# Output projection and first layer norm: applying the norm of one token group inside the matmul loop of the next

## The reference

```python
def _layernorm(x, axis=-1, eps=1e-5):
    m = jnp.mean(x, axis=axis, keepdims=True)
    v = jnp.var(x, axis=axis, keepdims=True)
    return (x - m) / jnp.sqrt(v + eps)

# x: (4, 4096, 4096)
x = _layernorm(x + _L0_attn_ref(x, ...))   # 8 heads of 64, ends in out @ Wo_w.T + Wo_b
x = _layernorm(x + _L0_ffn_ref(x, ...))    # dense 4096x4096 + top-2-of-8 LoRA experts
```

## Time and profile before

| | us |
|---|---|
| median of 13 runs | 4233.42 (4199.22 to 4473.61) |
| time of the profiled execution | 4216.77 |
| its span on the slowest core (core 7) | 4215.2 |
| spans of the 8 cores | 4149.0 to 4215.2 |
| busy on core 7: PE, DVE, ACT, POOL | 3192.0, 1367.2, 826.2, 714.9 |

### The profile page before, as it was taken

One profiled execution on the slowest core, in us unless ns is written; L12 is line 12 of the kernel. 1 busy time (PEld: TensorE's weight loads), 2 busy tenths in 40 slices (PEclk: granted clock), 3 DMA queues, 4 the chain that ended last, 5 costly groups with the idle time before them and its releaser, 6 DMA issues.

```text
span 4215.2 us, 46281 instructions; the slowest of 8 cores (4149.0 to 4215.2 us)
## 1 busy us (share of the span) xinstructions
PE 3192.0 (76%) x13476; PEld 1204.8 (29%) x13476; DVE 1367.2 (32%) x1908; ACT 826.2 (20%) x1412; POOL 714.9 (17%) x567
## 2 busy tenths in 40 slices
PE   4776795968888887888888655450799997999960
PEld 3555342412222222222222111110344442444420
DVE  0000000055566656566556235553100002111124
ACT  1222000013333333333333322110000000000000
POOL 2111101000000000000000013334222221444425
PEclk9998898956777767677767677775899998999985
DMA  8998545400000000000000142213554544666637
GB/s 245 284 280 263 158 137 167 135 11 1 1 1 3 1 1 1 3 1 1 3 1 1 36 132 75 80 40 98 175 160 148 162 133 155 201 209 204 208 116 191
DMA packets 450639, 444.75 MB, mean 106 GB/s; under 512 B 21472, under 2 KB 402529, under 8 KB 450402
## 3 DMA queue, kind: packets, MB, share of 16 engines
q1 hardware_dynamic: 347490, 341.12, 27.3%
q10 hardware_dynamic: 102912, 100.68, 7.4%
HBM read 340.01 MB, written 100.66 MB: 105 GB/s over the span
## 4 chain that ended last, share of the span: by engine, by line
PE 56%; DVE 9%; issue 6%; DMA 5%; POOL 3%; ACT 0%; DVEq 0%; SPq 0%; POOLq 0%; ACTq 0%
PE pf L155 23%; PE sS L155 10%; PE rb L155 9%; PE a L155 7%; DVE racc L557 4%; PE po L155 3%; DVE x2g L965 2%; DMA outT<-outst 2%; POOL tmpf L955 2%; PE pstQ L155 1%; PE pstS L155 1%; DMA wstgo<-woT 1%; PE pss L155 1%; PE sS L582 1%; PE psq L155 1%
## 5 line engine op out<-in xcount | busy, mean ns | idle before, releaser
L557 DVE TENSOR_REDUCE racc<-sS 128x1 f32<-128x512 f32 x1024 | 681.9, 689 | 1260.5 <-PE sS L155 1247.1
L155 PE MATMUL pf<-x2h,wqf 128*128 128x512 bf16 x4096 | 909.8, 380 | 5.8 <-DVE hs L1285 5.8
L703 ACT ACTIVATE probs<-rb 128x512 bf16<-128x512 f32 x1024 | 541.9, 598 | 913.1 <-PE rb L155 910.2
L155 PE MATMUL sS<-kT,qT 64*128 64x512 bf16 x1024 | 476.1, 484 | 155.9 <-DVE racc L557 118.9
L155 PEld LDWEIGHTS pf<-x2h,wqf 128*128 128x128 bf16 x4096 | 396.7, 98 | 505.7 <-issue 39.5
L155 PE MATMUL a<-probs,V 128*65 128x512 bf16 x1024 | 376.9, 495 | 0.0
L155 PE MATMUL pk<-xbf,wk_bf 128*128 128x256 bf16 x2048 | 264.2, 289 | 139.8 <-ACT xbf L333 60.5
L1310 POOL CAST wqf<-wstgf 128x1024 bf16<-128x1024 f32 x256 | 264.5, 1040 | 581.3 <-DMA wstgf<-wbT 419.3
L1376 DVE SCALAR_TENSOR_TENSOR res2c<-pf,bB_sb,x2h 128x1024 bf16<-128x1024 f32 x64 | 82.2, 1284 | 865.1 <-PE pss L155 793.3
L155 PE MATMUL rb<-qT,kT 64*128 64x512 bf16 x1024 | 339.8, 474 | 0.4 <-PE rb L155 0.2
L844 POOL CAST wo_bf<-wstgo 128x1024 bf16<-128x1024 f32 x16 | 16.6, 1040 | 1702.5 <-DMA wstgo<-woT 1702.5
(11 more groups left out here) (104 smaller groups left out, 1763.1 us busy)
## 6 DMA issues: line engine op xcount, KB each, us to landing
wstgf<-wbT SPq DMA_DIRECT2D x256, 512.0 KB
xstg<-xrot SPq DMA_DIRECT2D x128, 512.0 KB
xscr<-xbf ACTq DMA_DIRECT2D x128, 256.0 KB, 5.5
xvb<-xscr SPq DMA_DIRECT2D x128, 256.0 KB, 2.7
outT<-outst ACTq DMA_DIRECT2D x64, 512.0 KB, 4.7
xqb<-xscr SPq DMA_DIRECT2D x32, 512.0 KB, 3.4
xq<-xscr SPq DMA_DIRECT2D x32, 512.0 KB, 3.6
x2scr<-x2g ACTq DMA_DIRECT2D x32, 512.0 KB, 2.8
```

The costliest lines, as they stand in the source:

```text
L155: return lambda e: e.matmul(o, l, r, start=st, stop=sp, skip_group_check=True)
L557: e.reduce_max(d, srd, AX.X, negate=True),
L703: e.activation(d, srd, AF.Exp),
```

## The change

The apply loop is no longer emitted behind its own group. The broadcast with its two copies, each of the 32 apply steps and each of the 8 DMAs to `x2scr` becomes a closure in a list `opend`. In the matmul loop of the next group, every step takes two of them off the list before it emits its own matmuls: 41 closures, so the first 20 of the 32 steps take two each and the next takes the last one. What is left in the list after the fourth group is emitted behind the loop. Beside that, the `po` tiles go from two to three, the `sq` tiles from two to four, the statistics matmuls trail by three steps in place of one, and the weights are loaded and tracked by column block (`hh` outside, `c` inside), so that a step waits only for the quarter of `wo_bf` that it reads.

```diff
-                woR = [Res() for _ in range(4)]
+                woR = [[Res() for _ in range(4)] for _ in range(4)]
-                sq = sbP("sq", [128, 2 * 512], BF16)
+                sq = sbP("sq", [128, 4 * 512], BF16)
-                for c in range(4):
-                    for hh in range(4):
-                        st_i = hh % 2
+                for hh in range(4):
+                    for c in range(4):
+                        st_i = c % 2
...
-                    po = [po0, po1]
+                    po = [po0, po1, po2]
+                    opend = []
...
                         for mc in range(NDC):
-                            pi = mc % 2
+                            for _ in range(2):
+                                if opend:
+                                    opend.pop(0)()
+                            pi = mc % 3
...
-                                    woR[hp_].rd() + OTr[hp_][qg].rd(),
+                                    woR[hp_][mc // 8].rd() + OTr[hp_][qg].rd(),
...
+                            if len(ppend) > 2:
+                                emit_stats(*ppend.pop(0))
...
-                            sqi = mc % 2
+                            sqi = mc % 4
...
                             ppend.append((mc, te, ts, sqi))
-                            if len(ppend) > 1:
-                                emit_stats(*ppend.pop(0))
...
+                        def mk_bcast(ro=ro, trs=trs, tb2=tb2):
+                            def f():
+                                tba = s.op("PE", mm(pbc0[:], ones1f[:], ro(1),
...
+                        opend.append(mk_bcast())
                         for mc in range(NDC):
...
+                            def mk_apply(mc=mc):
+                                def f():
+                                    ti = mc % 2
+                                    t1 = s.op("POOL",
...
+                            opend.append(mk_apply())
+                            if mc % 4 == 3:
+                                def mk_spill(qg=qg, g=mc // 4):
...
+                                opend.append(mk_spill())
+                    while opend:
+                        opend.pop(0)()
```

More of the change, by code:

```diff
@@ L819, in build_program @@
                 resR = [Res() for _ in range(32)]
-                sq = sbP("sq", [128, 2 * 512], BF16)
-                sqR = [Res(), Res()]
+                sq = sbP("sq", [128, 4 * 512], BF16)
+                sqR = [Res() for _ in range(4)]
                 x2g = sbP("x2g", [128, 32 * 512], BF16)
@@ L949, in build_program @@
-                        bbcR.did_write(tcb)
-                        for mc in range(NDC):
[L951 to L981, removed]
+                        def mk_bcast(ro=ro, trs=trs, tb2=tb2):
+                            def f():
+                                tba = s.op("PE", mm(pbc0[:], ones1f[:], ro(1),
+                                                    True, True),
+                                           waits=[trs] + pbcR_[0].wr() +
+                                           consts_fence)
+                                rowsRes[1].did_read(tba)
+                                pbcR_[0].did_write(tba)
+                                tbb = s.op("PE", mm(pbc1[:], ones1f[:], ro(0),
+                                                    True, True),
+                                           waits=[tb2] + pbcR_[1].wr())
+                                rowsRes[0].did_read(tbb)
+                                pbcR_[1].did_write(tbb)
+                                tca = s.op("DVE", lambda e, d=abc[:], srd=pbc0[:]:
+                                           e.tensor_copy(d, srd),
+                                           waits=[tba] + abcR.wr())
+                                pbcR_[0].did_read(tca)
+                                abcR.did_write(tca)
+                                tcb = s.op("DVE", lambda e, d=bbc[:], srd=pbc1[:]:
+                                           e.tensor_copy(d, srd),
+                                           waits=[tbb] + bbcR.wr())
+                                pbcR_[1].did_read(tcb)
+                                bbcR.did_write(tcb)
+                            return f
@@ new lines, in build_program, with f @@
+                        opend.append(mk_bcast())
+                        for mc in range(NDC):
+                            def mk_apply(mc=mc):
+                                def f():
+                                    ti = mc % 2
+                                    t1 = s.op("POOL",
+                                              lambda e, d=tmpf[ti][:],
+                                              a=res[:, mc * 512: mc * 512 + 512],
+                                              b=abc[:]:
+                                              e.tensor_tensor(d, a, b, ALU.mult),
+                                              waits=resR[mc].rd() + abcR.rd() +
+                                              tmpfR[ti].wr())
+                                    resR[mc].did_read(t1)
+                                    abcR.did_read(t1)
+                                    tmpfR[ti].did_write(t1)
+                                    t2 = s.op("DVE",
+                                              lambda e,
+                                              d=x2g[:, mc * 512: mc * 512 + 512],
+                                              a=tmpf[ti][:], b=bbc[:]:
+                                              e.tensor_tensor(d, a, b, ALU.add),
+                                              waits=[t1] + bbcR.rd() +
+                                              x2gR[mc].wr())
+                                    tmpfR[ti].did_read(t2)
+                                    bbcR.did_read(t2)
+                                    x2gR[mc].did_write(t2)
+                                return f
+                            opend.append(mk_apply())
+                            if mc % 4 == 3:
+                                def mk_spill(qg=qg, g=mc // 4):
+                                    def f():
+                                        tw = s.op("ACT",
+                                                  lambda e, qg=qg, g=g:
+                                                  e.dma_start(
+                                                      x2scr_r[
+                                                          :, 4 * g:4 * g + 4,
+                                                          qg * 512:
+                                                          qg * 512 + 512],
+                                                      x2g.ap().rearrange(
+                                                          "p (c n) -> p c n",
+                                                          c=32)[
+                                                          :, 4 * g:4 * g + 4, :]),
+                                                  waits=[tk for j in range(4)
+                                                         for tk in
+                                                         x2gR[4 * g + j].rd()],
+                                                  dma="sca")
+                                        for j in range(4):
+                                            x2gR[4 * g + j].did_read(tw)
+                                        x2scrR[qg].did_write(tw)
+                                    return f
+                                opend.append(mk_spill())
```

22 lines of the change are left out of this document (4 added, 18 removed).

## The result

The changed kernel takes 4122.88 us in the median of 11 runs, where 4119 were forecast. Over all runs that were compared, its time is 0.9756 of the kernel before, with a 95% interval of 0.9728 to 0.9784. In some executions of either kernel the cores of a die (0 to 3, or 4 to 7) run at a lower clock; every ratio here leaves these out, while the median of 11 runs includes two of them, and the other nine have 4113.31 in their middle. The profiled execution took 4113.44 us, 103.3 less than the one before; 104.6 were forecast for it.

A forecast was written before the change was run, and what follows sets the result against it. Apply and matmul loops, taking turns, bound the stage: 104.4 of 112.6 us a group. Three times 33.1 (99.3) plus 5.3 gave 104.6 off 4216.77, 4112.2; from the runs' middle, 4223.37, 4119. Range 4092 to 4173, the forecast's own 4100 to 4138.

The forecast's parts named there:

- What goes: Groups 2 to 4: apply and matmul loop together take 71.3 us in place of 104.4, 33.1 less a group.
- The 20 residual steps: Residual steps interleaved with the 32 applies: 2 us added to 52.6; contention rival 15 us, 4158 in all, chance 0.14.
- the nearer row: FFN residual operation beside POOL's weight cast, at its usual 1.28 and 1.04 us; taken as model for interleaved residual steps.
- the other end of the range: Interleaved residual steps all serial with the multiplies, contending like the add: 20 x 0.75 = 15 us; chance 0.14.
- the 1 us that would have spoken against the account: Interleaved steps: POOL idle longer than 1 us per pair would show the prediction wrong.
- The last 12 steps: Matmul-loop steps left without applies: 1.50 us a step, the loop ending at 69.3 before the clock allowance.
- the matmuls of steps 20 to 22 are done: At the end of residual step 19 (54.6), thanks to three po tiles; so step 23's matmuls start at 55.4.
- The clock: TensorE's granted clock: 2 us a group added in case the 12 steps without applies begin at the lower level.
- the sum of 71.3: Apply and matmul loop of one group together after the change: 69.3 plus 2 for the clock, in place of 104.4.
- The rival of a low clock: TensorE stays at the lower level through groups 2 to 4: only 16.4 us gained a group, 4169; chance 0.16.
- The first group: Group 1's matmul loop: step 31 starts at 2503.4 in place of 2508.66, a gain of 5.3 us.
- steps 4 to 6 are done on PE by then: Group 1, at residual step 4 (2466.53): step 7 then starts at 2467.4 and later steps take 1.50 each.

The follow-up runs named there:

- e2: Changed kernel with the deferral kept and the look-ahead taken back (two po and sq tiles, statistics one step late): interval 83.0 us, profiled execution 4123.31 us, no ratio.
- e3: Changed kernel with ScalarE copying each po tile to SBUF, so the residual step has two SBUF inputs: interval 89.6 us, ratio 0.9875 to the kernel before.
- e7: Changed kernel with the weights loaded in the old order, row block outside: interval 79.3 us, read by its trace alone.
- e4: Changed kernel with the add reading the broadcast row in PSUM, copy to bbc left out: ratio 0.9597 to the kernel before, median 4059.5 us.

## Why the prediction came out

- **What goes.** One apply loop beside one matmul loop, three times: forecast 33.1 a group, measured 112.8 - 79.3 = 33.5. e2 shows that the deferral carries 29.8 of it. That forecast and measurement agree so closely is in part luck, as the next three points show.
- **The 20 residual steps.** Put at 2 us, between -4 and 15. In the changed kernel residual step 19 ends 55.6 after the first multiply, against 52.6 + 2: 3 us. The choice of the nearer row (one input in PSUM, rows 6 and 7) was right, and e3 shows that the other end of the range is something that does happen, although not all of its 89.6 - 79.3 = 10.3 us need be contention. POOL waited 14.3 us for adds in this part, 0.89 a pair, under the 1 us that would have spoken against the account. The Trainium skill (SBUF — State Buffer, Who interferes with whom) says that a VectorE instruction with two SBUF inputs contends with a GpSimd instruction that reads SBUF, the later one waiting for the whole of the earlier, and that one with at most one such input, outside the two-port modes, doesn't; e3 and the changed kernel agree, up to 1652 ns with two and at most 752 with one.
- **The last 12 steps.** 1.49 a step against 1.50. The step that failed is "the matmuls of steps 20 to 22 are done": with three tiles only 20 and 21 are. (For the first group the same prediction counted rightly: step 7 starts when the tile of step 4 is free.) It cost 0.9 us (57.3 against 55.4, less the 1.0 by which residual step 19 was later).
- **The clock.** 2 us were put in for the case that the last 12 steps begin at the lower level, and none did: 1.00 there. The 0.95 of the interleaved part is a group's start: PE begins a group at the lower level, is busy without a break while it works ahead, and then has the upper level for the rest of the group. So the sum of 71.3 was met at 71.1 by luck, by two misses of opposite sign, 1.9 too little and 2 too much. The rival of a low clock is refuted: PE was busy for 27.84 of 48 us, in bursts, and stayed at the upper level. The Trainium skill (TensorE: Matmul & The Clock Gate, HAM oscillation) warns of matmuls in bursts, with waits for DMA between them, that start cold; pauses such as the 1.57 us ahead of 2573.49 and the 1.71 ahead of 2600.89 did not bring that, and the 1.67 and 2.96 us of e3, close behind each other, did.
- **The first group.** Forecast 5.3. First load to broadcast copy is 107.5, and it was 114.1 before (core 7: its stage begins at 2403.83, its first multiply at 2518.74, 0.8 behind the copy): 6.6. Here too two misses cancel, as the rows shown with e7 tell. The forecast left residual step 4 at 2466.53, because it waited for `xq`. But its own matmuls had ended only 0.17 us before that (2465.32 + 1.04), so PE paced it as well, and with the look-ahead it comes 5.9 us behind the first residual step in place of 9.3, 3.4 earlier (the row names `xq` again, but there too its matmuls had ended only 0.18 before, at 2495.69). From there to residual step 31 it takes 40.3 us in place of 43.3, a gain of 3.0 and not 5.3: "steps 4 to 6 are done on PE by then" failed, since step 5's matmuls begin only at 2496.15. Over the eight cores, first load to copy is 110.5 to 114.8 before and 101.4 to 107.6 now. That the weights' order brings nothing is shown by e7.
- **The rest.** The last apply loop stayed at 53 us, and nothing behind the barrier took the gain back: the sum of three times 33.5 and 6.6 is 107.1, and the profiled executions, on different cores, differ by 103.3.

## What to carry to other kernels

Two loops that use different engines and alternate behind each other gained 29.8 us a group here from running side by side, against 5 to 6 from the look-ahead within one of them, and a list of closures taken off in the next loop was enough for it. When an elementwise step is moved beside GpSimd work, look at where its inputs lie: with two of them in SBUF, VectorE's steps and GpSimd's multiplies took turns here; leaving one operand in PSUM (e4) was worth another 1.6% here, 0.9756 to 0.9597. And count accumulator tiles by the step that reuses them: with n tiles, step k + n starts when k is read, and isn't done then.

## What the runs showed that I had not expected

The exclusion works both ways, where I had expected one side or the other to grow: in e3 a residual step beside a multiply took 1.65 us and a multiply up to 1.61, where alone they take 0.75 and 1.15. Without a second SBUF input nothing of it is left: the multiply's spread over 128 instructions is 25 ns in e4. And TensorE kept the upper level (granted clock 1.00 from 2552 to 2600) through bursts of 1.02 us for a step's four matmuls with pauses such as 1.57 and 1.71 us ahead of them; in e3, behind pauses of 1.67 and 2.96 us, it fell to the lower one.
